# A decoder megakernel: rows, first tap and rectified step sizes made by ScalarE instead of VectorE in the state-space stretches

## The reference

```
x = x + cosine similarity of norm(x) with the context        # L0 cross
x = x + gated pair of experts of norm(x)                     # L0 ffn
xz = norm(x) @ in_proj.T + b;  x_, z = split(xz)             # L1 attention, state space
x_ = silu(conv4(x_) + conv_b)                                # 4 taps, causal, per channel
dt, B, C = split(x_ @ x_proj.T);  dt = softplus(dt @ dt_proj.T + dt_b)
dA = floor(exp(-dt*exp(A_log)) * 2^15) / 2^15
h_t = dA_t * h_{t-1} + dt*x_*B_t;  y = (h . C) + D*x_        # 16 states, 512 channels
x = x + (y * silu(z)) @ out_proj.T + b
x = x + cross attention (8 heads of 64) of norm(x);  x = x + MoE of norm(x)
```

## Time and profile before

| | |
|---|---|
| median of 3 runs | 2367.3 us (2364.72 to 2368.29) |
| the profiled execution | 2387.01 us, span 2384.8 us |
| PE busy | 2072.3 us, 87% |
| DVE (VectorE) busy | 1717.6 us, 72% |
| ACT (ScalarE) busy | 1045.8 us, 44% |
| POOL (GpSimd) busy | 334.0 us, 14% |
| state-space stretches with a head | 1104.8 to 1756.5 us of the span |

### The profile page before, as it was taken

One profiled execution on the slowest core, in us unless ns is written; L12 is line 12 of the kernel. 1 busy time (PEld: TensorE's weight loads), 2 busy tenths in 40 slices (PEclk: granted clock), 3 DMA queues, 4 the chain that ended last, 5 costly groups with the idle time before them and its releaser, 6 DMA issues.

```text
span 2384.8 us, 33574 instructions
## 1 busy us (share of the span) xinstructions
PE 2072.3 (87%) x12364; PEld 1260.1 (53%) x12364; DVE 1717.6 (72%) x2514; ACT 1045.8 (44%) x1641; POOL 334.0 (14%) x368
## 2 busy tenths in 40 slices
PE   6999999999999999885768887988788889839998
PEld 4666666666666666551323344444354445516665
DVE  6677777777777778869999899989998995210001
ACT  1223333322322222237765867587758872202221
POOL 1111111111111111100000000000000001362222
PEclk8999999999999999997789987989899999969999
DMA  6000000000000100011110111011101113112442
GB/s 242 2 0 19 28 26 1 18 28 26 1 18 10 50 2 1 1 38 47 49 60 19 44 52 42 19 36 60 35 19 43 53 36 116 49 26 62 125 124 49
DMA packets 62238, 99.80 MB, mean 42 GB/s; under 512 B 13332, under 2 KB 44591, under 8 KB 61584
## 3 DMA queue, kind: packets, MB, share of 16 engines
q1 hardware_dynamic: 55120, 90.10, 11.6%
q0 software_dynamic: 6976, 7.84, 1.7%
HBM read 83.53 MB, written 15.53 MB: 42 GB/s over the span
## 4 chain that ended last, share of the span: by engine, by line
PE 53%; DVE 28%; issue 10%; ACT 4%; DMA 2%; another core or an unknown queue 1%; POOL 0%; DVEq 0%; SPq 0%; ACTq 0%; POOLq 0%
PE po L1810 9%; PE pa L1800 9%; DVE arena L1561 8%; PE pa L1758 4%; PE po L2378 4%; DVE arena L1551 4%; PE pt L1775 3%; PE pa L2084 3%; PE pa L2367 3%; DVE arena L1158 2%; DVE arena L1569 2%; DMA arena<-rows_to_experts 2%; PE pa L1790 1%; DVE arena L1160 1%; PE pt L1783 1%
## 5 line engine op out<-in xcount | busy, mean ns | idle before, releaser
L2084 PE MATMUL pa<-arena 128*128 128x512 f32 x512 | 297.9, 711 | 85.8 <-DVE arena L1569 85.8
L1561 DVE TENSOR_TENSOR_SCAN arena<-arena 128x1024 f32<-128x1024 f32 x128 | 292.5, 2285 | 13.5 <-ACT arena L937 13.3
L580 POOL TENSOR_SCALAR arena<-arena 128x2 f32<-128x2 f32 (+1 forms) x92 | 27.4, 298 | 1528.2 <-DVE arena L1426 824.7
L1810 PE MATMUL po<-arena 128*128 128x256 f32 x960 | 224.2, 385 | 0.0
L2084 PEld LDWEIGHTS pa<-arena 128*128 128x128 f32 x512 | 100.8, 216 | 218.8 <-DVE arena L1569 117.4
L1800 PE MATMUL pa<-arena 128*128 128x512 f32 x480 | 212.5, 595 | 4.4 <-ACT arena L754 4.1
L776 ACT COPY arena<-pa 128x512 f32<-128x512 f32 x128 | 65.7, 600 | 324.1 <-PE pa L1758 324.1
L1233 DVE TENSOR_TENSOR arena<-pa,arena 128x512 f32<-128x512 f32 x256 | 158.7, 682 | 63.1 <-PE pa L1758 63.0
L921 ACT ACTIVATE arena<-arena 128x510 f32<-128x510 f32 x256 | 170.7, 718 | 55.1 <-DVE arena L1561 51.8
L1810 PEld LDWEIGHTS po<-arena 128*128 128x128 f32 x960 | 176.8, 189 | 32.9 <-issue 6.0
L1701 DVE TENSOR_TENSOR arena<-po,arena 128x512 f32<-128x512 f32 x14 | 9.7, 692 | 231.2 <-PE po L2378 231.2
(11 more groups left out here) (268 smaller groups left out, 3706.6 us busy)
## 6 DMA issues: line engine op xcount, KB each, us to landing
arena<-bc_rows SPq DMA_DIRECT2D x64, 512.0 KB, 4.2
arena<-in_L_ffn_W SPq DMA_DIRECT2D x16, 1024.0 KB, 8.7
arena<-in_L_attn_W SPq DMA_DIRECT2D x8, 1024.0 KB, 5.5
rows_to_experts<-arena SPq DMA_DIRECT2D x4, 1024.0 KB, 13.0
arena<-rows_to_experts SPq DMA_DIRECT2D x8, 512.0 KB
out<-arena SPq DMA_DIRECT2D x5, 512.0 KB, 8.7
arena<-in_x SPq DMA_DIRECT2D x4, 512.0 KB, 7.0
arena<-in_rows SPq DMA_DIRECT2D x8, 256.0 KB, 3.2
```

The source lines that it names most:

```text
L1561: v.tensor_tensor_scan(h.rearrange(flat), decay.rearrange(flat), h.rearrange(flat), 0.0, ALU.mult, ALU.add).then_inc(scan_done, 1)
L1810: last = mm(po[s][:, ts(i, D)], gT[:, c, ts(tile, P)], w2[:, c, :], start=c == 0, stop=c == FM - 1)
L2084: last = mm(pa[c][:, :], ident, uh[i % len(uh)][:, n, :], start=g == 0 and n == 0, stop=g == NS // NG - 1 and n == NG - 1)
```

## The change

ScalarE takes three things from VectorE. First, in stretches with a scan and a head the normalised rows: `scaled(k)` on ScalarE in its slots 2, 10 and 23, at the end of the slot's decay and cross work, four activations Identity(rstd * x + nmr) of 128x256, where `nmr` = -mean * rstd. GpSimd's `shifts` makes it, with two more instructions (a negation before the add and the power, a product after them) before `rstd_ready` is signalled. Second, the first tap of the convolution: four activations Identity(w * x + b) of 128x512 after `x_half(3)`, ahead of `conv_silu(0)`; VectorE's three other taps of a chunk wait for it (`tap_ready`). Third, the rectified step sizes: four activations Relu(bank + dt_b) of 128x512 on ScalarE after the two exponentials, ahead of `z_half(2)`. VectorE's marks per head go from 45 to 41, and the arena grows by eight columns. The head of pair 0, which runs beside the last attention layer, keeps its rows on VectorE.

```diff
@@ -46,7 +46,7 @@
 ATTN_STEPS, FFN_STEPS = 4, 12
 BLOCKS, SLOTS = 6, 12
 END_STEPS, HEAD_ALONE = 5, 28
-HEAD_STEPS, TAIL_STEPS, CROSS_STEPS = 45, 5, 6
+HEAD_STEPS, TAIL_STEPS, CROSS_STEPS = 41, 5, 6
 ACT_STEPS = 2 * UNITS
 CROSS_SLOTS = 38
 ROUTED_EARLY = 36
@@ -209,7 +209,7 @@
     ts = bass.ts
 
 
-    ARENA = 51 * 1024 + 576
+    ARENA = 51 * 1024 + 576 + 2 * TT
     arena = ctx.enter_context(nc.sbuf_tensor("arena", [P, ARENA], F32))
     keep = Arena(arena, 0)
     xst = keep(NT, D)
@@ -217,6 +217,7 @@
     const = keep(C_ALL)
     stats, mv, ve, rstd = keep(TT, 6), keep(TT, 2), keep(TT), keep(TT)
     lgall = keep(NT, 8)
+    neg, nmr = keep(TT), keep(TT)
     ident, tri = const[:, C_ID:C_ID + P], const[:, C_TRI:C_TRI + P]
     strict, ones = const[:, C_STRICT:C_STRICT + P], const[:, C_ONES:C_ONES + P]
     mhalf, slot0 = const[:, C_MHALF:C_MHALF + TT], const[:, C_SLOT:C_SLOT + 8]
@@ -401,6 +402,7 @@
     u_ready, dtx_ready = sem("u_ready"), sem("dtx_ready")
     at2T_done, at2T_out = sem("at2T_done"), sem("at2T_out")
     xr_ready = sem("xr_ready")
+    nmr_ready, tap_ready = sem("nmr_ready"), sem("tap_ready")
     soft_e_ready, soft_u_ready, abs_ready, relu_ready = sem("soft_e_ready"), sem("soft_u_ready"), sem("abs_ready"), sem("relu_ready")
 
     logits_ready, sel_ready, rank_done, lt_ready, gexp_ready, places_ready = (
@@ -579,6 +581,15 @@
             hold(pool, var_ready, n)
             step.apart(nc.gpsimd.tensor_scalar(ve[:, c:c + k], mv[:, c:c + k, 1], LN_EPS, None, ALU.add))
             nc.gpsimd.tensor_tensor(rstd[:, c:c + k], ve[:, c:c + k], mhalf[:, 0:k], ALU.pow).then_inc(rstd_ready, 1)
+
+        def shifts(n, done):
+
+            hold(pool, var_ready, n)
+            nc.gpsimd.tensor_scalar(neg, mv[:, :, 0], -1.0, None, ALU.mult).then_inc(nmr_ready, 1)
+            step.apart(nc.gpsimd.tensor_scalar(ve, mv[:, :, 1], LN_EPS, None, ALU.add))
+            nc.gpsimd.tensor_tensor(rstd, ve, mhalf, ALU.pow).then_inc(nmr_ready, 1)
+            hold(pool, nmr_ready, done)
+            nc.gpsimd.tensor_tensor(nmr, neg, rstd, ALU.mult).then_inc(rstd_ready, 1)
 
         nc.gpsimd.memset(zero, 0.0).then_inc(zero_ready, 1)
         hold(pool, const_in, 16)
@@ -672,7 +683,7 @@
                 send_rows(0, NT - TT, 1)
             if n is not None and p is not None:
                 for k in range(3):
-                    deviations(GROUPS + groups + k + 1, 0, TT)
+                    shifts(GROUPS + groups + k + 1, 6 * p + 2 * k + 2)
             more = 3 if n is not None else 0
             if p is not None:
                 deviations(GROUPS + groups + more + 1, 0, TT)
@@ -860,9 +871,21 @@
                     act.wait_ge(head_v, HEAD_V * n + 4 + i)
                     a_(eb[:, i, :], eb[:, i, :], ACT.Silu).then_inc(sil_ready, 1)
 
+            def scaled(k):
+
+                if k == 0:
+                    hold(act, tail_tr, p)
+                hold(act, rstd_ready, GROUPS + 3 * heads + tails + ends + k + 1)
+                for i in range(TT):
+                    last = a_(xn[:, i, :], xst[:, bass.ds(n * TT + i, 1), :].rearrange("p a d -> p (a d)"), ACT.Identity,
+                              scale=rstd[:, i:i + 1], bias=nmr[:, i:i + 1])
+                last.then_inc(xn_ready, 1)
+
             def head(i):
                 if i == 2:
                     text()
+                if p is not None and i in (2, 10, 23):
+                    scaled((2, 10, 23).index(i))
                 if i == 3:
                     root(1, tn)
                 if i in (4, 5):
@@ -891,6 +914,14 @@
             def z_half(c):
                 act.wait_ge(in_done, 8 * n + IC + c + 1)
                 a_(zs[:, c, :], z_banks[c][:, :], ACT.Silu, bias=in_b[:, IC + c:IC + c + 1]).then_inc(in_out, 1)
+
+            def first_tap(c):
+
+                act.wait_ge(in_out, 8 * n + c + 1)
+                if p is not None:
+                    act.wait_ge(yg_ready, IC * p + c + 1)
+                a_(xs[:, c, :].rearrange("p (s t) -> p s t", s=2), xpad[:, c, :, KCONV - 1:KCONV - 1 + S], ACT.Identity,
+                   scale=cw[:, c, KCONV - 1:KCONV], bias=conv_b[:, c:c + 1]).then_inc(tap_ready, 1)
 
             def conv_silu(c):
                 act.wait_ge(conv_ready, IC * n + c + 1)
@@ -1013,6 +1044,8 @@
                 if p is not None:
                     act.wait_ge(ysum_done, UNITS * p + UNITS)
                 x_half(3)
+                for c in range(IC):
+                    first_tap(c)
                 conv_silu(0)
             if p is not None and n is None:
                 last_out(len(LAST_SLOTS) - 1)
@@ -1036,6 +1069,8 @@
                 halves = [slice(0, IC // 2), slice(IC // 2, IC)]
                 for half in halves:
                     a_(soft_e[:, half], soft_e[:, half], ACT.Exp, scale=-1.0).then_inc(soft_e_ready, 1)
+                for c in range(IC):
+                    a_(dt[:, c, :], dt_banks[c][:, :], ACT.Relu, bias=dt_b[:, c:c + 1]).then_inc(relu_ready, 1)
                 z_half(2)
                 z_half(3)
             routed = LATE_X if q is not None and n is not None else 0
@@ -1481,9 +1516,7 @@
             def head(i):
                 if i == 0:
                     statistics(rows_of(n))
-                if i == 1:
-                    if p is not None:
-                        dve.wait_ge(tail_tr, p)
+                if i == 1 and p is None:
                     scaled(head_groups[0], rows_of(n), xnt).then_inc(xn_ready, 1)
                 if i == 3:
                     inverse(2, tn)
@@ -1496,7 +1529,7 @@
                     dve.wait_ge(head_v, HEAD_V * n + 2)
                     step.apart(v.tensor_tensor(xst[:, ts(n, TT), :], xst[:, ts(n, TT), :], dn, ALU.add))
                     statistics(rows_of(n))
-                if i == 9:
+                if i == 9 and p is None:
                     scaled(head_groups[1], rows_of(n), xnt).then_inc(xn_ready, 1)
                 if i == 13:
                     gate_logits()
@@ -1515,7 +1548,7 @@
                     pair_added(3)
                 if i == 21:
                     statistics(rows_of(n))
-                if i == 22:
+                if i == 22 and p is None:
                     scaled(head_groups[2], rows_of(n), xnt).then_inc(xn_ready, 1)
 
             if head_alone:
@@ -1569,15 +1602,12 @@
                 v.tensor_tensor(h, h, Cs[g % 2], ALU.mult).then_inc(hc_ready, 1)
 
             def convolved(c):
-                dve.wait_ge(in_out, 8 * n + c + 1)
+                dve.wait_ge(tap_ready, IC * n + c + 1)
                 dst = xs[:, c, :].rearrange("p (s t) -> p s t", s=2)
-                for tap in range(KCONV):
+                for tap in range(1, KCONV):
                     at = KCONV - 1 - tap
                     src, w_tap = xpad[:, c, :, at:at + S], cw[:, c, at:at + 1]
-                    if tap == 0:
-                        last = v.tensor_scalar(dst, src, w_tap, conv_b[:, c:c + 1], ALU.mult, ALU.add)
-                    else:
-                        last = v.scalar_tensor_tensor(dst, src, w_tap, dst, ALU.mult, ALU.add)
+                    last = v.scalar_tensor_tensor(dst, src, w_tap, dst, ALU.mult, ALU.add)
                     if tap < KCONV - 1:
                         step.after(last)
                 last.then_inc(conv_ready, 1)
@@ -1645,10 +1675,6 @@
                 scaled(tail_group + 1, rows, xnt).then_inc(xn_ready, 1)
             if q is not None:
                 statistics(rows_of(q))
-            if n is not None:
-                for c in range(IC):
-                    dve.wait_ge(abs_ready, IC * n + c + 1)
-                    v.tensor_scalar(dt[:, c, :], dt_banks[c][:, :], dt_b[:, c:c + 1], 0.0, ALU.add, ALU.max).then_inc(relu_ready, 1)
             if q is not None:
                 scaled(cross_group + 1, rows_of(q), [xr[:, i, :] for i in range(TT)]).then_inc(xr_ready, 1)
             if n is not None:
```

## The result

The changed kernel takes 2402.7 us (median of 4 runs, 2400.95 to 2403.43) against 2367.8 (4 runs, 2364.72 to 2369.21): ratio 1.0139, 95% interval 1.0118 to 1.0159. It is slower, as forecast, but by five times as much: +35 us where the working had +7.1, and outside the range.

The account below looks back on a forecast made before the run. VectorE's list bounds loop p=0, a three-engine chain parts of loops p=1 and p=2, TensorE fed by ScalarE the closing parts. First part +3.2 +1.9, loops -3.7 -0.8 -0.8, closes +1.9 +2.4 +3.0: +7.1, 2374.4 us; range 2366 to 2380.5.

Parts of the forecast that it names:

- GpSimd's two additions: At the head's norms, GpSimd's negation before and product after the power: 1.2 us for both, ScalarE's rows starting at 1115.4.
- The 0.4 us of room before scan 3: In loop p=0, ScalarE's decay stands at 1119.6 and the scan wants 1119.99, so it just fits, by 0.4.
- -3.7: Loop p=0: moving the rows off VectorE gains 3.7 of the possible 3.87 us.
- -0.8 each: Loops p=1 and p=2: moving the rows gains 0.8 us each, bounds the full 3.87 and a loss of 1.
- if GpSimd's product took over 2 us: One of three stated conditions, at the head's norms, under which the forecast would be wrong.
- the power's 2.76 as its upper bound: At the head's norms, GpSimd's product lasts at most 2.76 us; then loop p=0 would still gain some 2.
- Half clock: Rival: TensorE falls to 1.2 GHz at gaps before routed rows, 2 us each, first closing part 1 more; +12, 2379; chance 0.15.
- First tap and rectification in the first part: First closing part: the tap delays the last convolution chunk by +3.2 us, the rectification delays the first logarithm by +1.9.
- the tap was put at zero: Later closing parts: the tap's delay, up to 2.8 us each, is covered by TensorE's projection, so zero.
- the rectification at 1.9, 2.4 and 3.0: Later closing parts: rectifying on ScalarE delays queries by +1.9 us, then routed rows by +2.4 and +3.0.
- The rival with all gains: Rival: ScalarE and GpSimd never late, three loops give 3.87 us each; sum +0.8, 2368; chance 0.27 with its neighbourhood.

Follow-up runs that it names:

- e7: Against the kernel before: only the normalised rows on ScalarE, GpSimd keeping its two instructions and VectorE making the shift column; 2364.1 us, ratio 0.9982.
- e14: Kernel of e1 with GpSimd's four instructions reordered to add, power, negation, product; 2364.3 us, ratio 0.9981 against the kernel before.
- e15: The whole change with GpSimd's order of e14 and three matmuls filling TensorE's gap before the routed rows; 2374.3 us, ratio 1.0012.
- e12: The kernel before, unchanged, run again for a second profile; 2371.3 us.
- e6: The whole change with three extra TensorE matmuls filling the gap before the routed rows; 2392.0 us, ratio 1.0091 against the kernel before.
- e8: The whole change with TensorE's gap filled and the shift column made by VectorE instead of GpSimd; 2369.6 us, ratio 1.0002.
- e13: Kernel of e1 with VectorE waiting behind each of the head's statistics until GpSimd's chain is done; 2382.8 us, ratio 1.0058 against the kernel before.
- e5: The whole change, unaltered, run again for the spread of its executions; 2399.6 us, ratio 1.0109 against the kernel before.
- e2: Against the kernel before: only the first tap moved to ScalarE, behind the fourth eviction; 2373.9 us, ratio 0.9998.
- e3: Against the kernel before: only the rectified step sizes moved to ScalarE; 2382.7 us, ratio 1.0067.
- e11: Kernel of e3 with three spare matmuls filling TensorE's gap before the routed rows; 2379.3 us, ratio 1.0037 against the kernel before.
- e16: The whole change with GpSimd's order of e14, TensorE's gap left open; 2406.7 us, ratio 1.0090 against the kernel before in the same session.
- e9: Kernel of e7 with the first tap also on ScalarE, each tap right behind its own eviction; 2362.2 us, ratio 0.9966 against the kernel before.
- e1: Against the kernel before: only the normalised rows moved to ScalarE, with GpSimd's two further instructions; 2381.8 us, ratio 1.0045.
- e10: Kernel of e1 with four spare GpSimd instructions a scan ahead of each loop's second and third chain; 2383.5 us, ratio 1.0052 against the kernel before.

## Why the prediction was wrong

**GpSimd's two additions: the step that failed.** It took 1.2 us, with "ordinary arithmetic and the power is the costly one". They cost 3.6 at the three norms of loop p=0 (chain 7.6 against 3.9). The 0.4 us of room before scan 3 was gone six times over: ScalarE took up the rows at 1119.30, 13.1 us behind the first scan, where 10.6 was reckoned (1115.4). Loop p=0 came to +2.5 instead of -3.7, and with the chain mended it has 163.2 (e7, e14, e15), -4.0. Loops 1 and 2 came to +3.6 and +11.0 against the first profile of before and to 0.0 and +8.1 against e12, instead of -0.8 each, and not all of that is the chain's (below). In the whole change with the gap filled the chain is worth 0.0079 by its order (e6 against e15) and 0.0089 where GpSimd keeps its two instructions (e6 against e8): 19 to 21 us of the 33 that the ratio of the change says. I had named "if GpSimd's product took over 2 us" and the power's 2.76 as its upper bound. But at that bound I reckoned a gain of some 2 left in loop p=0: I charged the product alone, and not the negation ahead, which pushes every later instruction onto another of VectorE's. The product itself took 1.56 us on average. The bound was wrong because 2.76 was no price: the trace of before has the same power at 1.04 where VectorE stands idle.

```profile
1321.62 1.19 DVE L1569 TENSOR_TENSOR arena<-arena 128x1024 f32<-128x1024 f32 x1
1321.90 1.00 POOL L580 TENSOR_SCALAR arena<-arena 128x4 f32<-128x4 f32 x1 [8.04 <-DVE arena L1426]
1323.08 1.04 POOL L581 TENSOR_TENSOR arena<-arena 128x4 f32<-128x4 f32 x1 [0.18 <-POOL arena L580]
1325.91 2.29 DVE L1561 TENSOR_TENSOR_SCAN arena<-arena 128x1024 f32<-128x1024 f32 x1 [3.09 <-ACT arena L937]
```

The Trainium skill states the rule (SBUF — State Buffer, section SBUF: two separate sides): VectorE and GpSimd share a port pair, and a VectorE instruction with two SBUF inputs, if it has started first, holds it for its whole length against a GpSimd one that reads SBUF. e13 and e14 agree with it, with 2.15 and 5.4 us.

**Half clock: right mechanism, too small.** It was a rival, priced at 2 us a gap and +12 in all. It came in the close 1-2, at the gap named, in all three profiles of the whole change with the gap open, and took 9.2 us there (62.8 against 53.6): the slow pace lasted some 24 us, over the keys and queries, not "the next few microseconds". In the close 2-3 it did not come. In time the filled gap is worth 4 to 11 us (e5 and after against e6).

**First tap and rectification in the first part:** +3.2 and +1.9 reckoned; e2 has 2.2, e3 2.0, after 3.5 for both (37.9 from the fourth `x_half` to the first scan against 34.4). But this part itself varies: e12 has 33.2, e11, with e3's first part, 34.5 for 36.4, and e8 39.9. So 1.9 us can't be confirmed there. In the later closes the tap was put at zero and showed 2.9 and 1.8 in e2; the rectification at 1.9, 2.4 and 3.0 showed 1.8, 2.5 and 1.4 in e3 (the close 2-3 of before varies by 1.0, see e12).

**The sum without the two faults.** With the chain in order and the gap filled the whole change is at +2.8 us (e15, -1.7 to +7.3) or +0.5 (e8, -2.6 to +3.6). The rival with all gains, +0.8, lies in both intervals, the forecast's +7.1 only just in the first. So that the change came out slower, as forecast, is luck as far as the sum goes: its terms leave nothing clear of noise, and the loss as measured is that of the two faults, of which only the half clock was among the rivals. One thing I haven't settled: loop 2 has 194.8 to 199.5 us in the kernels with the rectification and no long chain (e3, e8, e11, e15, e16), though nothing in it changed but its start, and 190.6 to 194.4 in those without (before, e12, e2, e7, e9, e14). The rectification may cost a few microseconds there that the forecast doesn't have.

## What to carry to other kernels

Where one kind of instruction has two durations in one trace, find what runs beside it before using either as a price: here a small GpSimd instruction lasted at least as long as what was left of VectorE's product or scan at its start, so its cost depends on where in VectorE's list it falls, and the order of a few such instructions can be worth more than moving work (e14 against e1, 15 us by the ratios for one line moved). A wait of some microseconds placed in TensorE's dense list should be filled or priced with the clock behind it. A producer for the first use belongs right behind its own input, not behind all four (e9).

## What the hardware showed

- GpSimd's four instructions on 128x4 take 0.24, 0.23, 1.04 and 0.20 us beside an idle VectorE, and 1.01, 2.05, 1.81 and 2.26 beside its products and scans; idle time ahead (8 to 83 us in e13) plays no part.
- Beside VectorE's instructions with one tile operand GpSimd was not held (0.23, 1.17 and 0.20 us in e10). Nor was a power that started at 1220.39, 0.02 us behind one of VectorE's short two-operand instructions (0.49 us long): 1.03 us.
- The same gap of 2.85 us in TensorE's list lowered the clock in the close 1-2 (0.81) and not in the close 2-3 (1.00) of one execution, and so again in two others (e5, e16).
- One chip ran the kernel before at 2385.0 us, where the other sessions had 2368 to 2370. No profile of that kernel was kept there; e16's has 422.8 us behind the last scan, some 20 more than the others.
